# Relation products kept as two exact float32r parts, gathered as 2 KB rows and summed by single-pass one-hot products

## What is computed

```python
W = jnp.einsum('rb,bio->rio', comp, basis)          # 8 relations from 4 bases
H = jnp.einsum('ni,rio->nro', x, W)                 # x: the normalised nodes
msg = H[src, etypes]                                # one row of 256 per edge
agg = jax.ops.segment_sum(msg, dst, num_segments=N_NODES)
out = agg + x @ loop_weight + bias_param
```

## Time and profile before

| | us |
|---|---|
| Median of 3 runs (lowest to highest) | 2128.86 (2124.54 to 2131.22) |
| Span of the profiled execution | 2334.4 |
| PE busy (matmul) | 2035.6 (87%) |
| DVE busy | 1287.5 (55%) |
| POOL busy | 1033.4 (44%) |
| ACT busy | 783.0 (34%) |

### The profile page before, as it was taken

How to read it: one execution, slowest core, us unless ns; L and a number is a source line. 1 busy time by engine, 2 the same in 40 slices (tenths; PEclk the granted TensorE clock), 3 DMA queues, 4 the chain that set the end, 5 groups by cost and what they waited for, 6 DMA issues and landing times. The chain is left out here.

```text
span 2334.4 us, 29468 instructions
## 1 busy us (share of the span) xinstructions
PE 2035.6 (87%) x8898; PEld 1313.2 (56%) x8898; DVE 1287.5 (55%) x2800; ACT 783.0 (34%) x2025; POOL 1033.4 (44%) x1084
## 2 busy tenths in 40 slices
PE   7999967888888888599785888888888989999999
PEld 3456633434444446499643566566666955565565
DVE  7696635666766665433365677777677832112121
ACT  4322222222222313243345454445442333322322
POOL 5687855666666540333266566556554410000000
PEclk9999978999999998699897899999889989999999
DMA  4158432322323321622247676667663300000000
GB/s 129 40 108 123 119 105 79 86 84 84 90 83 91 82 64 46 219 73 72 75 145 207 185 208 194 185 195 202 186 183 98 109 1 1 9 10 1 9 10 8
DMA packets 116242, 233.21 MB, mean 100 GB/s; under 512 B 26975, under 2 KB 71142, under 8 KB 113398
## 3 DMA queue, kind: packets, MB, share of 16 engines
q0 software_dynamic: 53168, 151.69, 23.5%
q1 hardware_dynamic: 62918, 79.64, 12.3%
HBM read 190.44 MB, written 40.67 MB: 99 GB/s over the span
## 5 line engine op out<-in xcount | busy, mean ns | idle before, releaser
L2634 PE MATMUL p_ag<-rows_g,oh_g 128*128 128x260 f32 x1408 | 394.8, 429 | 86.5 <-issue 43.7
L2271 POOL DMA_INDIRECT rows_g<-g_table,row_src x352 | 334.7, 951 | 234.7 <-issue 92.1
L948 POOL DMA_INDIRECT rows<-h_table,row_rel x352 | 337.7, 959 | 214.0 <-issue 89.4
L2634 PEld LDWEIGHTS p_ag<-rows_g,oh_g 128*128 128x128 f32 x1408 | 266.6, 207 | 182.4 <-issue 94.7
L3001 DVE SCALAR_TENSOR_TENSOR x<-p_yf,cw_f,x 128x256 f32<-128x256 f32 (+1 forms) x160 | 66.4, 477 | 281.3 <-PE p_yf L3161 281.3
L2385 DVE TENSOR_TENSOR rows_g<-rows_g,p_e 128x2048 f32<-128x2048 f32 x88 | 200.1, 2274 | 3.9 <-issue 3.9
L1280 PE MATMUL p_agg<-rows,oh 128*128 128x256 f32 x704 | 192.1, 414 | 1.9 <-issue 1.8
L402 POOL DMA_INDIRECT slot_table<-rec_f,dst_i x120 | 164.6, 1372 | 39.4 <-issue 39.4
L1073 DVE TENSOR_TENSOR fT<-a_sb,p_sel 128x512 f32<-128x512 f32 x200 | 128.5, 682 | 92.2 <-DMA xT_table<-xT 47.1
L1280 PEld LDWEIGHTS p_agg<-rows,oh 128*128 128x128 f32 x704 | 136.0, 204 | 62.1 <-issue 42.1
L3161 PE MATMUL p_yf<-f,h_f 128*128 128x256 f32 (+1 forms) x640 | 148.4, 386 | 0.8 <-ACT h_f L3053 0.8
(11 more groups left out here) (517 smaller groups left out, 3542.4 us busy)
## 6 DMA issues: line engine op xcount, KB each, us to landing
h_table<-h_out SPq DMA_DIRECT2D x20, 1024.0 KB
where_g<-d_table SPq DMA_DIRECT2D x88, 128.0 KB
w<-in_L_ffn_W SPq DMA_DIRECT2D x16, 512.0 KB, 9.6
y_table<-yb_g SPq DMA_DIRECT2D x47, 128.0 KB, 1.7
rows<-h_table,row_rel POOLq DMA_INDIRECT x352
rows_g<-g_table,row_src POOLq DMA_INDIRECT x352
g_table<-row SPq DMA_DIRECT2D x20, 260.0 KB
f<-in_L_ffn_W SPq DMA_DIRECT2D x16, 256.0 KB, 7.2
```

The lines of the kernel that those rows point to most:

```text
L948: pool.indirect_dma_start(rows[:, r, j], None, st.h_rows, bass.IndirectOffsetOnAxis(ap=st.row_rel[:, at:at + 1], axis=0)).then_inc(gathere ...
L2271: pool.indirect_dma_start(rows[:, r, j], None, st.g_table, bass.IndirectOffsetOnAxis(ap=st.row_src[:, at:at + 1], axis=0)).then_inc(gather ...
L2634: last = pe.matmul(p_a[:, k % NS, h, 0:HALF], oh[:, r, j], rows[:, r, j, h * HALF:(h + 1) * HALF], start=j % w == 0, stop=j % w == w - 1)
```

## The change

In `slots_and_front` the table row of a relation becomes 2 KB: a float32r part (the product rounded by ScalarE's copy) and the exact rest (product minus that part, a new DVE instruction on PSUM, `low_part`). `h_out` is cut into four places, one for each bank q, each with both parts of two relations (4 KB to a partition), and is stored in four DMAs of 512 KB to a tile. In `mix0_and_gather` the indirect DMAs gather 2 KB rows, the ring of rows has four places, and each column is summed by two float32r products (one-hot by first part, one-hot by rest). One-hots are written as float32r. The ring of one-hots stays at six.

```diff
+HQ = 4
-        h_out = sb("h_out", [P, 2, R * D])
+        h_out = sb("h_out", [P, HQ, R // HQ, 2, D])
...
-        h_stored = [sem(f"h_stored{u}") for u in range(2)]
+        h_rest = sem("h_rest")
+        h_stored = [sem(f"h_stored{q}") for q in range(HQ)]
...
+        h_parts = st.h_table.rearrange("n (q d) -> n q d", q=HQ)
...
             for t in range(T):
-                sp.wait_ge(h_copied, 4 * (t + 1))
-                sp.dma_start(st.h_table[t * P:(t + 1) * P, :], h_out[:, t % 2]).then_inc(h_stored[t % 2], 16)
+                for q in range(HQ):
+                    sp.wait_ge(h_rest, HQ * t + q + 1)
+                    sp.dma_start(h_parts[t * P:(t + 1) * P, q], h_out[:, q].rearrange("p r c d -> p (r c d)")).then_inc(h_stored[q], 16)
                 if t + XR < T:
                     load(t + XR)
...
+            def low_part(t, q):
+                dve.wait_ge(h_copied, 4 * t + q + 1)
+                dve.tensor_tensor(h_out[:, q, :, 1].bitcast(F32R), p_h[q].rearrange("p (r d) -> p r d", r=2), h_out[:, q, :, 0],
+                                  ALU.subtract).then_inc(h_rest, 1)
...
             for t in range(T):
                 hots(t, t % 2)
+                for q in range(4):
+                    if t:
+                        low_part(t - 1, q)
                 if t == SQ_AT + 4:
                     mixing_constants()
...
+            for q in range(4):
+                low_part(T - 1, q)
...
-                for q in range(4):
-                    act.wait_ge(h_ready, 4 * t + q + 1)
-                    nc.scalar.copy(h_out[:, t % 2, q * 512:(q + 1) * 512], p_h[q]).then_inc(h_copied, 1)
+                for q in range(HQ):
+                    if t:
+                        act.wait_ge(h_stored[q], 16 * t)
+                    act.wait_ge(h_ready, HQ * t + q + 1)
+                    nc.scalar.copy(h_out[:, q, :, 0].bitcast(F32R),
+                                   p_h[q].rearrange("p (r d) -> p r d", r=2)).then_inc(h_copied, 1)
...
                 for q in range(4):
                     if t:
-                        pe.wait_ge(h_copied, 4 * (t - 1) + q + 1)
+                        pe.wait_ge(h_rest, 4 * (t - 1) + q + 1)
...
     RING = 6
+    ROWS = 4
-        rows = sb("rows", [P, RING, BATCH, D])
+        rows = sb("rows", [P, ROWS, BATCH, 2, D])
...
-                if s >= RING:
-                    pool.wait_ge(agg_done, GR * (s - RING + 1))
+                if s >= ROWS:
+                    pool.wait_ge(agg_done, GR * (s - ROWS + 1))
...
-                    last = pe.matmul(p_agg[:, k % 3, at:at + D], oh[:, r, j], rows[:, r, j], start=j % w == 0, stop=j % w == w - 1)
+                    for c in range(2):
+                        last = pe.matmul(p_agg[:, k % 3, at:at + D], oh[:, s % RING, j].bitcast(F32R), rows[:, r, j, c].bitcast(F32R),
+                                         start=j % w == 0 and c == 0, stop=j % w == w - 1 and c == 1)
...
-        st.h_table = nc.dram_tensor("h_table", (NP, R * D), F32).ap()
+        st.h_table = nc.dram_tensor("h_table", (NP, R * 2 * D), F32).ap()
```

More of the change, by code:

```diff
@@ L8 @@
 I32 = mybir.dt.int32
+F32R = mybir.dt.float32r
 ALU = mybir.AluOpType
@@ L209, in slots_and_front @@
         loop_p = sb("loop_p", [P, 2, D])
-        h_out = sb("h_out", [P, 2, R * D])
-        basis = h_out[:, 0].rearrange("p (b k o) -> p b k o", b=NB, k=K)
-        w_lv = h_out[:, 1, 0:K * 2 * D].rearrange("p (k o) -> p k o", k=K)
-        w_qk = h_out[:, 1, K * 2 * D:].rearrange("p (k o) -> p k o", k=K)
+        h_out = sb("h_out", [P, HQ, R // HQ, 2, D])
+        h_flat = h_out[:, :, :, :, :].rearrange("p q r c d -> p (q r c d)")
+        basis = h_flat[:, 0:NB * K * D].rearrange("p (b k o) -> p b k o", b=NB, k=K)
+        w_lv = h_flat[:, NB * K * D:NB * K * D + K * 2 * D].rearrange("p (k o) -> p k o", k=K)
+        w_qk = h_flat[:, NB * K * D + K * 2 * D:].rearrange("p (k o) -> p k o", k=K)
         comp = sb("comp", [P, R * NB])
@@ L329, in _ @@
             for t in range(T):
-                sp.wait_ge(h_copied, 4 * (t + 1))
-                sp.dma_start(st.h_table[t * P:(t + 1) * P, :], h_out[:, t % 2]).then_inc(h_stored[t % 2], 16)
+                for q in range(HQ):
+                    sp.wait_ge(h_rest, HQ * t + q + 1)
+                    sp.dma_start(h_parts[t * P:(t + 1) * P, q], h_out[:, q].rearrange("p r c d -> p (r c d)")).then_inc(h_stored[q], 16)
                 if t + XR < T:
                     load(t + XR)
-            for u in range(2):
-                sp.wait_ge(h_stored[u], 16 * (T // 2))
+            for q in range(HQ):
+                sp.wait_ge(h_stored[q], 16 * T)
         @block.gpsimd
@@ L713, in _ @@
             for t in range(T):
-                if t >= 2:
-                    act.wait_ge(h_stored[t % 2], 16 * (t // 2))
                 if t == 0:
                     act.wait_ge(w_rel_ready, 1)
-                for q in range(4):
-                    act.wait_ge(h_ready, 4 * t + q + 1)
-                    nc.scalar.copy(h_out[:, t % 2, q * 512:(q + 1) * 512], p_h[q]).then_inc(h_copied, 1)
+                for q in range(HQ):
+                    if t:
[3 more added lines that the diff above has]
+                                   p_h[q].rearrange("p (r d) -> p r d", r=2)).then_inc(h_copied, 1)
                 if t == SQ_AT:
@@ L907, in mix0_and_gather @@
         agg_added = sem("agg_added")
-        gathered = [sem(f"gathered{r}") for r in range(RING)]
+        gathered = [sem(f"gathered{r}") for r in range(ROWS)]
         block = ctx.enter_context(nc.Block())
@@ L942, in _ @@
             for s in range(NBATCH):
-                r = s % RING
-                if s >= RING:
-                    pool.wait_ge(agg_done, GR * (s - RING + 1))
+                r = s % ROWS
+                if s >= ROWS:
+                    pool.wait_ge(agg_done, GR * (s - ROWS + 1))
                 for j in range(BATCH):
                     at = FIRST_COLUMN[s] + j
-                    pool.indirect_dma_start(rows[:, r, j], None, st.h_rows,
+                    pool.indirect_dma_start(rows[:, r, j].rearrange("p c d -> p (c d)"), None, st.h_rows,
                                             bass.IndirectOffsetOnAxis(ap=st.row_rel[:, at:at + 1], axis=0)).then_inc(gathered[r], 16)
@@ L1188, in one_hot @@
                 act.wait_ge(away_ready, n + 1)
-                nc.scalar.activation(oh[:, s % RING], away[:, :, :], ACT.Relu, bias=one[:, 0:1], scale=-1.0).then_inc(oh_made, 1)
+                nc.scalar.activation(oh[:, s % RING].bitcast(F32R), away[:, :, :], ACT.Relu, bias=one[:, 0:1], scale=-1.0).then_inc(oh_made, 1)
             def take_kv(p):
@@ L1267, in one_sum @@
             def one_sum(s, g):
-                r, w = s % RING, WIDTH[s]
+                r, w = s % ROWS, WIDTH[s]
                 k = GROUP[s] + (g if w < BATCH else 0)
```

4 lines of the change are left out of this document (2 added, 2 removed).

## The result

| | us |
|---|---|
| Before, median of 4 runs (lowest to highest) | 2128.14 (2124.54 to 2131.22) |
| Changed, median of 4 runs | 2158.68 (2157.33 to 2163.52) |
| Ratio | 1.0152, 95% interval 1.0133 to 1.0171 |
| Span of the profiled execution, changed | 2156.2 |
| Forecast | 2097 (2070 to 2138) |

The kernel became 30 us slower. The forecast was 32 us faster, and the result lies outside its range.

A forecast was written before the change was run, and what follows sets the result against it. PE was taken to bound the front loop and to be the busiest engine, not alone, in the gather stage. From 2128.86 us, +15 (subtractions) + 0 (stores) - 47 (sums) = -32 gave 2097 us, range 2070 to 2138.

The forecast's parts named there:

- What bounds the kernel now: Front loop bound by PE; in the 566 us gather stage PE is the busiest engine but not alone.
- Part 1: Front loop: 80 new DVE subtractions stall PE 6.0 us before tile 1 and lengthen DVE tiles to 11.1 us; +15 us.
- The waits of about 1 us: Front loop, tiles 1 to 9: DVE's 11.1 us a tile against PE's 10.15, nine times 0.95, 8.6 us.
- Part 2: Front loop stores: 2 MB a tile in four 512 KB pieces stay hidden, 0; bound +44 us if slow tiles double.
- rival 1: Front loop: ACT's copies wait for stores, DVE and PE behind; +44 us, giving 2141; chance 0.18.
- Part 3: Gather stage sums: float32r saves 0.84 us a batch, 74 us of PE work, of which 47 us shorten the time.
- Part 4: Gather stage: 352 issues as before, now for 2 KB rows with a ring of four, add nothing; 0.
- rival 3: Gather stage: gather issuing bounds it, query blocks shorten by half, giving 2122; chance 0.08.
- What would show it: Signs: right by PE stalls and a stage of some 515 us; wrong by ACT store waits, sums 0.21 us apart, PE awaiting rows.
- The last sign: Gather stage: a granted clock below 0.92, since PE has more gaps, would give part of the gain back.

The follow-up runs named there:

- half_store: Changed kernel storing and gathering only the first parts (1 MB a tile, 1 KB rows), subtractions kept, second product with zeros: 2130.5 us, ratio 1.0017 to before.
- no_low: Changed kernel without the VectorE subtractions, rests being zeros written once, same 2 MB a tile stored: 2142.4 us, ratio 1.0069 to before.
- no_low_deep6: Changed kernel with six places in h_out instead of four and no subtractions, rests being zeros, still 2 MB a tile: 2127.8 us, ratio 1.0008 to before.
- sums_only: Kernel before with only the sums changed to two float32r products, the second with zeros, all gathers of 1 KB rows: 2116.4 us, ratio 0.9958.
- one_product: Kernel before with each column summed by a single float32r product, all 352 gathers kept, rests left out: 2121.7 us, ratio 0.9970.
- contig_store: Changed kernel with the table laid out bank by bank, each store filling one contiguous block: 2164.1 us, ratio 1.0158 to before.
- pair_store: Changed kernel with two stores of 1 MB to a tile, 8 KB pieces, instead of four of 512 KB: 2161.9 us, ratio 1.0172 to before.

## Why the prediction was wrong

**What bounds the kernel now.** Right for the front loop. Wrong for the gather stage: "PE is the busiest engine but not alone" was seen, and then GpSimd was set aside by a stage length of 566 us from an execution that I knew to be 205 us too long. From first to last gather that profile has 540 us, the later one 452. Even the rows at hand held a warning: a keys part of 35.15 us has seven batches, and seven batches at 5.0 us of issuing are 35.0.

**Part 1, `low_part`: +15.** Right in size and mechanism. 13 us of the front by `half_store` and by the difference to `no_low` (13.8 and 15.2 us of the loop), with the stall of 5.75 us and the DVE tile of 11.0 us where they were foretold. The waits of about 1 us stand in `half_store` alone, seven of them and not nine; in the changed kernel the stores hide them. A part of the agreement is luck: 3 of `half_store`'s 13.8 us are PE busy for longer, a term that the sum does not have.

**Part 2, the stores: 0. This step failed.** `half_store` prices them at 31.8 us of the front. The mechanism of rival 1, with its place on ScalarE's copy, was right, and its +44 too high by 12; its chance of 0.18 was too low. The choice was argued from the fastest stretch, though the same rows showed the same bytes at a share of 0.85. The 410 GB/s of that stretch are no rate to count on: the row has a DMA share of 1.64 for its one microsecond, and over ten microseconds there the rows have 107 GB/s at a share of 0.39, an estimated 274 at a full share. `no_low_deep6` has 230 GB/s at 1.00. (By the prediction's own count of five slow and four middling tiles, eleven are fast, not twelve.) And the burst was allowed 10 us, while the store of tile 1's first bank was issued 7.0 us after its copy began. What neither Part 1, nor Part 2, nor the rival has is PE's clock: each counts a stall by its length alone, and after the six long stalls PE lost 15 us more.

**Part 3, the sums: -47. This step failed too.** It rested on three factors. The price of a batch: 0.84 us less forecast, 0.73 measured in a query block (1.79 to 1.06, each in one piece), nearly right. The share of it that shortens a stage that only PE and DVE hold: -47 forecast, -35 measured with half of the gathers. And the cover, which was put at nothing: with all the gathers it is 9 us, for 440 us of issuing fill 452, and PE stands 27.6 us before its sums instead.

**Part 4, the gathers: 0.** The 2 KB rows and the ring of four cost nothing, as said: GpSimd waits 4.0 us for sums. But the gathers hold the stage, as in rival 3, and leave 9 us of the 35 that the cheaper sums are worth without them. The price of rival 3, half of the saving kept, was still too mild.

**The sum by measured terms:** +13 (subtractions) + 32 (stores) - 9 (sums) = +36, against +30 in the medians and +35 between the two profiles. The 32 us of the stores hold PE's slower stretches. Rivals 1 and 3 came together. The cases were weighed as if only one could hold, and their sum lay at 2129 + 15 + 44 - 22 = 2166, beyond the range.

**What would show it.** The ScalarE waits and the GpSimd row were named as signs against the forecast, and both appeared. PE waiting for rows, the other half of the sign of rival 3, is put down to "issue" by the profile and to the gathers for 1.2 us only. The last sign was a granted clock below 0.92; by that number it did not appear. But the 0.92 was of the first profile. Against the second the clock did fall: it is 0.94 in the gather stage (361 to 811 us) where it is 0.99 in before, and PE's busy time falls only by 41 us (428 to 388) although its sums take 61 less (177.6 and 116.3 us busy by their line).

## What to carry to other kernels

Work is worth what the next limit leaves of it: before costing a saving on one engine, count the other engine's instructions by their spacing (352 times 1.25 us) and hold that against the stage of an execution whose span fits the median; a profile that does not fit is no scale, whatever factor it is multiplied with. Doubling the bytes of a store while keeping the buffer memory halves the places in time, and each wait put between a copy and its store comes off what is left. Sum up the waits of the engine that is full, not those of an engine with slack, and look at the pace after a stall as well as at its length. When two mends give little each, try them together before calling the resource exhausted.

## What had not been expected of the hardware

- Float32r records of 256 columns start 0.12 us apart in a batch at full granted clock (`sums_only`, 507.34 to 507.69 us), 0.46 ns a column, where the float16 matmuls take 0.42 ns. A whole batch of eight takes 1.06 to 1.20 us where eight float32 records take 1.79 to 1.93.
- After each of six stalls of 3.3 to 5.8 us in the changed kernel's loop, TensorE took 5.4 to 6.7 us for eight records that take 3.6 at full granted clock, 15 us in all.
- The granted clock of the gather stage falls with TensorE's work: 428 us busy at 0.99 in before (316 to 772 us), 388 at 0.94 in the changed kernel (361 to 811), 365 at 0.91 in `one_product` (314 to 772).
- The DMA engines carry 230 GB/s for 185 us at a share of 1.00 in `no_low_deep6`, and 188 GB/s at 0.83 in the changed kernel (120 to 345 us). Small scatters beside them take 9.3 us to land in `no_low_deep6` and 4.5 in before.
- Stores of 512 KB in pieces of 4 KB at a stride of 16 KB land in 7.0 us in the median (changed kernel), as contiguous blocks in 7.4 (`contig_store`), and stores of 1 MB in pieces of 8 KB in 8.5 (`pair_store`).
